# A gated delta rule kernel whose slot of 223 steps is written in another order

## What is computed

```python
q, k, v = x @ w_q, x @ w_k, x @ w_v                 # then a causal convolution of 4 taps, silu
beta = sigmoid(x @ w_b) * 2.0
g = -exp(A_log) * softplus(x @ w_a + dt_bias)
q, k = l2norm(q), l2norm(k)
# per head, token by token:
S = S * exp(g_t)
mem = einsum('bhk,bhkv->bhv', k_t, S)
delta = (v_t - mem) * b_t
S = S + einsum('bhk,bhv->bhkv', k_t, delta)
o_t = einsum('bhk,bhkv->bhv', q_t * scale, S)
# then
y = rms(o) * norm_w * silu(x @ w_g)
return y @ w_out
```

## Time and profile before

| | us |
|---|---|
| median of 3 runs | 5266.25 (5263.24 to 5266.33) |
| the profiled execution, its own time | 5268.2 |
| its span, first to last instruction | 5267.0 |
| PE busy | 4934.9 (94%) |
| DVE busy | 4242.5 (81%) |
| ACT busy | 3366.1 (64%) |
| POOL busy | 3077.9 (58%) |

### The profile page before, as it was taken

One profiled execution on the slowest core, in us unless ns is written; L12 is line 12 of the kernel. 1 busy time (PEld: TensorE's weight loads), 2 busy tenths in 40 slices (PEclk: granted clock), 3 DMA queues, 4 the chain that ended last, 5 costly groups with the idle time before them and its releaser, 6 DMA issues. The chain is left out here.

```text
span 5267.0 us, 151694 instructions
## 1 busy us (share of the span) xinstructions
PE 4934.9 (94%) x44556; PEld 3852.8 (73%) x44556; DVE 4242.5 (81%) x10169; ACT 3366.1 (64%) x10076; POOL 3077.9 (58%) x4419
## 2 busy tenths in 40 slices
PE   6699999999999999999999999999999999996998
PEld 6477777777777777777777777777777777774554
DVE  5588888888888888888888888888888888885775
ACT  1477777777677767777677767777777767762221
POOL 3566666666566666666666666666666666663443
PEclk9899999999999999999999999999999999998998
DMA  4111111011011011011111011011011111000110
GB/s 144 65 40 34 36 40 41 31 38 44 30 38 38 28 46 38 28 38 40 34 38 38 33 42 38 28 38 46 28 38 38 36 38 38 30 29 23 40 40 32
DMA packets 116451, 208.30 MB, mean 40 GB/s; under 512 B 12409, under 2 KB 70914, under 8 KB 116354
## 3 DMA queue, kind: packets, MB, share of 16 engines
q1 hardware_dynamic: 116354, 207.09, 11.5%
HBM read 187.65 MB, written 19.40 MB: 39 GB/s over the span
## 5 line engine op out<-in xcount | busy, mean ns | idle before, releaser
L656 DVE SCALAR_TENSOR_TENSOR cv<-ps_a,wqkv,cv 128x511 f32<-128x511 f32 (+2 forms) x1536 | 1142.4, 744 | 73.1 <-ACT cv L649 39.8
L641 PE MATMUL ps_a<-xin,wqkv 128*128 128x512 f32 x2048 | 1003.4, 613 | 33.4 <-POOL m L1124 31.1
L860 POOL TENSOR_TENSOR bm<-bat,mask 128x256 f16<-128x256 f32 x1536 | 1032.8, 694 | 0.0
L910 ACT ACTIVATE m<-b 128x256 f16<-128x256 f32 x1536 | 569.3, 388 | 424.7 <-PE b L905 424.5
L921 DVE TENSOR_TENSOR tt<-tt,b 128x256 f16<-128x256 f16 x1536 | 615.3, 414 | 95.1 <-PE b L916 74.7
L963 ACT CAST tt<-bu 128x256 f16<-128x256 f32 x1536 | 572.0, 372 | 134.7 <-PE bu L958 116.9
L1063 POOL TENSOR_TENSOR rms<-msq,epsq 128x2 f32<-128x2 f32 x512 | 99.7, 195 | 920.9 <-ACT sqo L1058 920.9
L641 PEld LDWEIGHTS ps_a<-xin,wqkv 128*128 128x128 f32 x2048 | 363.0, 192 | 291.9 <-issue 285.2
L1095 PE MATMUL ps_a<-wout,yT 128*128 128x256 f32 x2048 | 558.0, 395 | 0.5 <-ACT yT L1089 0.5
L837 DVE SCALAR_TENSOR_TENSOR bat<-ps_a,w,dec 128x256 f32<-128x256 f32 x1024 | 445.0, 476 | 114.0 <-PE ps_a L824 114.0
L905 PEld LDWEIGHTS b<-tt,bm 128*128 128x128 f16 x6144 | 348.8, 98 | 234.7 <-issue 191.7
(11 more groups left out here) (207 smaller groups left out, 12495.8 us busy)
## 6 DMA issues: line engine op xcount, KB each, us to landing
xin<-xT_scratch SPq DMA_DIRECT2D x128, 512.0 KB, 3.3
grow<-g_scratch SPq DMA_DIRECT2D x128, 512.0 KB, 4.0
gam<-g_scratch SPq DMA_DIRECT2D x256, 96.0 KB, 2.8
n_x<-in_x SPq DMA_DIRECT2D x16, 512.0 KB, 3.5
xT_scratch<-n_xT SPq DMA_DIRECT2D x16, 512.0 KB, 2.6
e_x<-in_x SPq DMA_DIRECT2D x16, 512.0 KB, 4.1
out_y<-e_yo SPq DMA_DIRECT2D x16, 512.0 KB, 2.9
wqkv<-in_w_qkv SPq DMA_DIRECT2D x32, 128.0 KB, 3.2
```

The costliest lines, as they stand in the source:

```text
L641: ins = pe.matmul(ps[:], wqkv[:, k, j * P:(j + 1) * P], xin[p][:, k, :], start=k == 0, stop=k == KT - 1)
L656: s.done(dve.scalar_tensor_tensor(y[:, r:], ps[:, 0:T - r], tap[:, j, TAPS - 1 - r:TAPS - r], y[:, r:], ALU.mult, ALU.add), f"a_tap{j}{r}")
L860: s.done(pool.tensor_tensor(half_of(bm[:, l, units(g), :], l, 1), half_of(bt[:, units(g), :], l, 1), half_of(c["mask"][:, l, :].unsqueeze( ...
L910: s.done(act.mul(half_of(m1[:, l, units(g), :], l, 0), half_bank(bank, l), -1.0), f"b_Me{l}{g}")
```

## The change

The table of a slot is another one: the same 223 steps in another order, 60 of them with another lag (b_g1, the fp16 levels 2 to 4 of the first half and a_proj2 and a_proj3, for instance, now stand at a lag one higher, b_kT, b_sq0 and b_eps at one lower). No operation and no `s.need` is changed; since `Banks` reads the table, who waits for whom at a bank changes with it. Both tables have a largest lag of 3. Of each table the lines with b_kk1 and with c_out2 (one line before, two now) and the first:

```diff
-    b_kT.1 b_V40.2 b_U11.2 a_tap32.1 b_Ve11.2 c_yTe1.3 c_SU2.3 a_tap33.1 b_bm31.2 b_sq0.1 c_O2.3 b_Ve40.2 b_M21.2
+    b_n0.1 b_Me01.2 a_tanh0.1 a_silu0.1 b_M20.2 c_O1.3 b_V01.2 b_Ve01.2 b_Me20.2 b_ss.1 c_sq1.3 b_Ue10.2 a_proj3.1
...
-    b_eps.2 b_sq1.1 c_O3.3 c_sq3.3 c_out2.3 c_acc2.3 b_diag0.1 c_m3.3 b_t20.1 c_p3.3 b_kk1.1 b_M41.2 b_T0.2 b_n1.1
+    b_kk1.1 b_vtok1.1 b_F0.2 b_g0.1 b_Ve41.2 b_tg0.1 b_T0.2 b_t20.1 b_ev11.1 b_Ue41.2 c_p3.3 b_bm00.1 b_bm10.1
...
+    b_V51.2 c_out2.3 b_sq1.1 b_U51.2 c_yTe3.3 b_Ue51.2 b_M00.1 b_Ve51.2 c_SU0.2 b_P1.2 a_tap12 c_O0.2 b_bm20.1
```

More of the change, by code:

```diff
@@ L68 @@
-    b_Ue30.1 c_p1.2 c_KS2.2 b_sg1.1 a_silu2 a_cv3 c_y1.2 c_R2.2 b_Me40.1 b_M11.1 b_U01.1 b_Ue01.1 c_out0.2 c_Z2.2
-    c_yT1.2 b_lo1.1 b_Me11.1 b_V11.1 a_tap31 c_u2.2 b_bm21.1
+    b_n0.1 b_Me01.2 a_tanh0.1 a_silu0.1 b_M20.2 c_O1.3 b_V01.2 b_Ve01.2 b_Me20.2 b_ss.1 c_sq1.3 b_Ue10.2 a_proj3.1
+    b_V20.2 b_U01.2 b_E0.1 c_S1.3 c_out0.3 b_Ue01.2 b_rc.1 c_m1.3 b_Ve20.2 c_p1.3 b_M11.2 c_y1.3 a_cv3.1 b_E1.1
+    b_lo0.2 c_KS2.3 b_Me11.2 b_M30.2 b_U20.2 b_Ue20.2 c_acc0.3 a_tap31.1 c_R2.3 c_yT1.3 a_proj2.1 b_bm40.2 b_V11.2
@@ new lines @@
+    c_Z2.3 c_yTe1.3 b_bm21.2 b_bm31.2 b_Me30.2 b_hi1.2 a_tap32.1 b_w1.1 a_tap33.1 a_cv2.1 b_Ve11.2 b_kw.1 c_u2.3
+    b_root.1 b_V30.2 b_U11.2 b_M21.2 b_lo1.2 b_Ve30.2 a_tanh3.1 a_tap21.1 b_bm41.2 b_Ue11.2 a_silu3.1 c_SU2.3
+    b_M40.2 b_Me21.2 a_tap22.1 b_bm51.2 c_O2.3 b_Me40.2 b_U30.2 b_V21.2 b_ktok.1 a_tap23.1 b_Ue30.2 c_out1.3
+    b_V40.2 c_S2.3 c_sq2.3 b_U40.2 c_m2.3 b_Ve21.2 b_bm50.2 b_Ue40.2 b_g1.2 c_acc1.3 b_Ve40.2 a_tanh2.1 b_U21.2
+    c_KS3.3 a_silu2.1 b_tg1.2 c_p2.3 c_y2.3 c_R3.3 b_M50.2 b_M31.2 b_kk0.1 b_Ue21.2 b_Me31.2 b_V31.2 b_Me50.2
@@ new lines @@
+    b_V50.2 b_sg1.2 b_U31.2 c_Z3.3 c_yT2.3 b_vT1.1 b_gam.1 b_Ue31.2 b_Ve31.2 b_Ve50.2 c_u3.3 c_yTe2.3 b_U50.2
+    b_M41.2 b_Me41.2 b_ev00.1 b_Ue50.2 b_P0.2 c_O3.3 b_U41.2 b_ev01.1 b_V41.2 c_sq3.3 b_R0.2 c_m3.3 b_diag0.1
+    b_kk1.1 b_vtok1.1 b_F0.2 b_g0.1 b_Ve41.2 b_tg0.1 b_T0.2 b_t20.1 b_ev11.1 b_Ue41.2 c_p3.3 b_bm00.1 b_bm10.1
+    b_M51.2 b_Me51.2 b_ev10.1 a_proj1 b_Tq0.1 a_cv1 c_Z0.2 c_y3.3 b_Tf0.1 c_yT3.3 b_sg0.1 a_tap11 b_qT.1 c_u0.2
+    b_V51.2 c_out2.3 b_sq1.1 b_U51.2 c_yTe3.3 b_Ue51.2 b_M00.1 b_Ve51.2 c_SU0.2 b_P1.2 a_tap12 c_O0.2 b_bm20.1
@@ L70 @@
+    c_acc2.3 b_Me00.1 b_n1.1 b_V00.1 a_proj0 b_bm30.1 b_gend.1 a_tap13 b_diag1.1 c_sq0.2 a_tanh1 b_U00.1 b_kqs.1
+    c_m0.2 c_p0.2 b_R1.2 b_Ve00.1 b_F1.2 c_S0.2 b_eps.1 b_M10.1 a_silu1 c_y0.2 a_cv0 c_KS1.2 b_T1.2 b_Me10.1
+    b_vT0.1 c_out3.3 c_R1.2 a_tap01 b_t21.1 c_Z1.2 b_vtok0.1 b_Ue00.1 b_bm01.1 b_hi0.1 a_tap02 b_Tq1.1 b_V10.1
+    c_u1.2 b_Tf1.1 b_Ve10.1 a_tap03 c_yT0.2 b_U10.1 b_kT b_bm11.1 c_SU1.2 c_yTe0.2 b_sel b_sq0 b_M01.1 c_acc3.3
 """.split()
```

## The result

The changed kernel takes 5286.63 us (median of 7 runs, 5282.09 to 5288.78) against 5266.25 (7 runs, 5261.29 to 5269.28): ratio 1.0039, 95% interval 1.0027 to 1.0051. The forecast was 5155. The profiled execution took 5288.78, its span is 5287.5.

The account below looks back on a forecast made before the run. TensorE (PE) was taken to bound the kernel, at 35.6 us a slot. Ordinary slots -99, pair changes -15 and depth +3 make -111 us: 5268.2 becomes 5157, or 5155 as median; range 5105 to 5215.

Parts of the forecast that it names:

- slots above 35.2: Sign that the prediction is wrong: slots staying above 35.2 us, where slots near 34.8 were expected.
- Waits that go: PE's waits in an ordinary slot, at b_kk1 and around b_V21: all 1.49 us were to go.
- the big one: PE's b_kk1 (L824), directly behind c_out2, waits for DVE's accumulate c_acc2: a loss of 1.0 us a slot.
- Waits that come: Three round trips too short in the new order, together between 0.20 and 0.40 us a slot; 0.3 taken.
- (a): PE's c_SU2 needs ACT's c_u2, which stands directly behind a_cv2: late by 0.20 us.
- (b): PE's b_M21 needs DVE's b_Ve11: 0.98 us against 0.88 between them, late by 0.10.
- (c): PE's b_M40 needs b_Ve30: the same 0.98 us against 0.88, late by 0.10.
- Tightness: On PE, fp32 steps behind fp16 steps are 0.083 us longer; five more such boundaries cost 0.42 us a slot.
- Rival 4: Boundaries cost nothing, as fp32 weights load ahead during the fp16 step: 5102 us; chance 0.05.
- An ordinary slot: Changes by -1.49 + 0.3 + 0.42 = -0.78 us; 127 of them give -99 us.
- Pair changes: Every 16th slot loads new weights and is 3.1 us too long, seven times (22 us); 1.0 expected after, -15 us.
- Rivals 1 to 3: DVE's queue takes half back, 5205 (0.15); DVE steps 0.1 us apart, about 5347; x tile late, about 5305 (together 0.07).

Follow-up runs that it names:

- act_shift40: The changed kernel with 40 idle wait instructions on ACT ahead of the loop; 5183.44 us, ratio 0.9848 to the kernel before.
- edge_moved: The changed kernel's table turned by 13 steps, putting the loop's edge at a_proj3's long matmuls, with 30 idle ACT instructions ahead; 5147.61 us, ratio 0.9781.
- before_out2_first: The kernel before with c_out2 and c_acc2 two steps earlier, ahead of c_O3 and c_sq3; 5190.48 us, ratio 0.9862.
- u2_first: act_shift40 with c_u2 ahead of a_cv2 on ACT; 5198.08 us, ratio 0.9878 to the kernel before.
- su2_behind_m40: edge_moved with b_M40 ahead of c_SU2 on TensorE; 5167.25 us, ratio 0.981 to the kernel before.

## Why the prediction was wrong

**Where it failed.** The prediction said "I take 35.6" for a slot and then: "It moves steps on four engines. No instruction is added or taken away." The sum followed from that, one ordinary slot 127 times. That step is false for a loop: what stands at its edge, and where each engine's body lies in its instruction stream, are moved as well, and I charged nothing for either. "No instruction is added or taken away" is not so of what is built: the profiled execution has 151288 instructions instead of 151694, and ACT's body 282 instead of 284. The runs price both terms that were put at nothing. ACT's stall at the edge: 103 us (act_shift40 against the change; 108.9 in the distances of the profiled executions, some 6 of it the clock). PE's gap at the edge: 34.9 us (edge_moved against act_shift40). Without them the same cycle of steps takes 5147.61 us, near the forecast of 5155. Neither was among the rivals, and the range ended at 5215. Of the signs that the prediction named, slots above 35.2 is the one that came: every second slot was above it.

That the stall hangs on the place of ACT's loop is shown by runs in both directions. That its cause is the count of blocks the body lies in fits them all, but is not shown. The number of instructions ahead of the loop was to be had from the built kernel; that it mattered was in no row of the trace before, where ACT's branch took 0.26 us.

**Waits that go, 1.49.** Right in kind: L824's row is gone, and b_V21 no longer waits. before_out2_first shows that the big one, reckoned at 1.0, was worth 0.6 to 0.8 when taken away alone, since other gaps come up behind it.

**Waits that come, 0.3.** The size was near: b_M21 to c_SU2 takes 0.49 for 0.12, so 0.37 (the row of waits has 30.8 us in 119 times). The parts were not, so this is in part luck. (a) was put at 0.20 and is all of the 0.37, and u2_first shows that it is the bare round trip and not a_cv2's place in ACT's queue. (b) and (c) were put at 0.10 each, with round trips of 0.98 against 0.88 of work. They take 0.90 or less (b_V11 to b_M21 in act_shift40) and 0.89 (b_V30 to b_M40 in su2_behind_m40), so they cost 0.01 or so; in the changed kernel L905 waits for L921 only 7 times.

**Tightness, 5 x 0.083.** One boundary measured 0.055 by itself, 0.08 at a projection. The term stands, perhaps a third too large. Rival 4 is refuted: a boundary is not free here. So where the Trainium skill, "TensorE: Matmul & The Clock Gate", section "Step-by-step: what each phase is for", says that the next tile's weights load while this tile's matmul runs, the trace shows that this does not hide all of it for steps as short as these. That it is the weights that take these 0.055 us was argued from step lengths; no run separates it.

**An ordinary slot.** Forecast 34.8; it is 34.73. From edge_moved: (4535.1 - 4410.8 - 13.8) / 127 = 0.87 won a slot instead of 0.78. With 1.49 gone and 0.37 come, 0.25 is left for the boundaries, 0.05 each, where 0.42 was charged: the mis-sized terms of the ordinary slot partly cancel.

**Pair changes.** In the kernel before these seven slots were 24.4 us too long (forecast 22), in edge_moved 10.6 (forecast 7). 13.8 won, 15 forecast. POOL's wait for grow is still there seven times, as foreseen, with 29.1 us in place of 64.8.

**Rivals 1 to 3** did not come up: no row shows L824 waiting for a_silu2 or L641 for xin, and DVE's instructions overlap as before.

## What to carry to other kernels

When a loop's body changes its order, look at the loop's edge apart from its middle: take slot lengths one by one, since 57 slots of about 37.1 hide behind 59 of 34.7 in any mean, and read "issue" rows whose count is that of the iterations. Where instruction fetches in the page rise between two versions of a loop (47 to 332 here), shift the engine's body by some idle instructions ahead of it before you judge the order; 40 of them were worth 2% here. Try the edge of a tight TensorE loop at long matmuls: here this took away 0.6 us an iteration, though the kernel before paid nothing for its edge among short steps. And read each step's neighbours on every queue that it is moved past: of the four reorderings that were tried on top of the changed table, each of which looked like a gain, three cost 15 to 84 us, and one won about 5 in its profile.
